# A ViT tower on one core: the FFN's up products reordered, and scores and turns moved ahead

## The reference

```
h = tok(x)                                   # patches projected, width 192
qkv = layernorm(h) @ W_qkv.T
att = softmax(8 * q @ k.T); o = att @ v      # inside one image, 36 x 36, 12 heads
h = h + cat(o) @ W_out.T
g = argmax(softmax(layernorm(h) @ gate_w + gate_b))
y = gelu(layernorm(h) @ w1[g] + b1[g]) @ w2[g] + b2[g]    # 192 -> 768 -> 192
out = h + y
```

## Time and profile before

| what | value |
|---|---|
| median of 3 runs | 298.41 us (297.48 to 299.12) |
| profiled execution | 296.83 us |
| its span, first to last instruction | 295.1 us |
| mean granted TensorE clock | 0.961 |
| PE busy | 270.5 us (92%) |
| DVE, ACT, POOL busy | 133.0, 127.2, 63.9 us |
| DMA mean | 80 GB/s |

### The profile page before, as it was taken

How to read it: one execution, slowest core, us unless ns; L and a number is a source line. 1 busy time by engine, 2 the same in 40 slices (tenths; PEclk the granted TensorE clock), 3 DMA queues, 4 the chain that set the end, 5 groups by cost and what they waited for, 6 DMA issues and landing times.

```text
span 295.1 us, 9448 instructions
## 1 busy us (share of the span) xinstructions
PE 270.5 (92%) x3858; PEld 243.8 (83%) x3859; DVE 133.0 (45%) x434; ACT 127.2 (43%) x362; POOL 63.9 (22%) x105
## 2 busy tenths in 40 slices
PE   7957989999999999999999987598999999999991
PEld 7937978899879999799998777496888888898890
DVE  6986067442575742774625742353223232232210
ACT  3463543634452725526444432304746355364330
POOL 2750001212002121012120001136052442533112
PEclk9985999999999999999999979869999999999998
DMA  6929900021950302000020000204012121121000
GB/s 247 286 59 429 413 22 2 13 114 51 420 234 4 125 0 60 4 2 4 2 62 3 2 4 2 60 0 130 7 53 67 40 55 58 47 48 42 10 0 0
DMA packets 5169, 23.47 MB, mean 80 GB/s; under 512 B 1383, under 2 KB 2675, under 8 KB 4878
## 3 DMA queue, kind: packets, MB, share of 16 engines
q1 hardware_dynamic: 3038, 18.48, 17.2%
q0 software_dynamic: 1792, 4.04, 5.0%
q10 hardware_dynamic: 304, 0.44, 0.5%
HBM read 20.30 MB, written 3.34 MB: 80 GB/s over the span
## 4 chain that ended last, share of the span: by engine, by line
PE 84%; DVE 6%; ACT 3%; issue 3%; POOL 1%; DMA 1%; POOLq 0%; DVEq 0%; ACTq 0%
PE psum L403 19%; PE psum L681 11%; PE psum L665 9%; PE psum L473 9%; PE psum L669 7%; PE psum L388 6%; PE psum L448 5%; PE psum L462 4%; PE psum L511 4%; PE psum L434 2%; PE psum L535 2%; PE psum L653 1%; PE psum L522 1%; DVE kT L943 1%; PE psum L396 1%
## 5 line engine op out<-in xcount | busy, mean ns | idle before, releaser
L862 ACT ACTIVATE kT<-psum,late 128x128 f32<-128x128 f32 x96 | 26.5, 375 | 43.8 <-PE psum L669 43.8
L403 PE MATMUL psum<-xn_hi,wq_parts 128*128 128x288 f32 x144 | 36.6, 324 | 3.0 <-DVE late_r L916 3.0
L1194 POOL TENSOR_SCALAR veps<-mv 96x1 f32<-96x1 f32 x24 | 5.3, 219 | 148.4 <-DVE mv L896 148.2
L681 PE MATMUL psum<-w2s,kT 128*128 x192 | 33.8, 327 | 0.0
L665 PE MATMUL psum<-qT,late 128*128 128x128 f32 x192 | 32.6, 292 | 0.0
L681 PEld LDWEIGHTS psum<-w2s,kT 128*128 128x128 f32 x192 | 30.8, 190 | 0.1
L403 PEld LDWEIGHTS psum<-xn_hi,wq_parts 128*128 128x128 f32 x144 | 26.4, 204 | 3.3 <-issue 3.3
L665 PEld LDWEIGHTS psum<-qT,late 128*128 128x128 f32 x192 | 25.8, 190 | 4.0
L403 PE MATMUL psum<-late_r,wq_parts 128*128 128x288 f32 x96 | 29.0, 310 | 0.0
L473 PE MATMUL psum<-wo,oT 128*96 128x192 f32 x144 | 27.3, 342 | 1.7 <-ACT oT L775 1.7
L403 PE MATMUL psum<-wq_parts,xn_hi 128*100 128x384 f32 x96 | 28.4, 350 | 0.0
(11 more groups left out here) (133 smaller groups left out, 473.5 us busy)
## 6 DMA issues: line engine op xcount, KB each, us to landing
w1s<-w_b SPq DMA_DIRECT2D x1, 4632.0 KB, 16.5
w2s<-w SPq DMA_DIRECT2D x1, 4608.0 KB, 15.7
xb<-xT SPq DMA_DIRECT2D x4, 864.0 KB, 4.5
token_table<-rows SPq DMA_DIRECT2D x3, 432.0 KB, 3.2
late<-w_proj SPq DMA_DIRECT2D x1, 960.0 KB, 4.9
b2s<-b SPq DMA_DIRECT2D x1, 768.0 KB, 17.8
wq_in<-w_qkv SPq DMA_DIRECT2D x1, 640.0 KB, 9.7
wo<-w_out SPq DMA_DIRECT2D x1, 576.0 KB
```

The lines of the kernel that those rows point to most:

```text
L403: mm = pe.matmul(dst, lhsT, rhs, start=(i == 0), stop=(i == len(parts) - 1))
L681: mm = pe.matmul(psum[:, Y_BANKS[i % 2], 0:D], hidT[i % 2][:, c * P:(c + 1) * P], w2s[:, bass.ds(e, 1), c, :], start=(c == 0), stop=(c == ...
L862: ge = act.activation(hidT[p2][:, c * P:(c + 1) * P], psum[:, 2 * p2 + c % 2, c // 2 * P:(c // 2 + 1) * P], ACT.Gelu, bias=w1_tile[i][:, U ...
```

## The change

Five edits. (1) `up` issues the 6 full-row products first and then the 6 half-row ones; for the first FFN tile the second tile's `turn_x` stands between the two. (2) `soften(1)` stands ahead of `normalise(0)` on DVE. (3) `scores(3)` stands ahead of the last `values`. (4) In the last block `turn_probs(3)` and `attend(2)` stand ahead of `project_to(0)`, and on ACT `take_attended(3)` ahead of `take_rows(0)`; the bank list follows. (5) 14 fillers instead of 24 ahead of the sorting product.

```
-FINAL = [("o", 0), ("gt", 0), ("o", 1), ("o", 2), ("gt", 1), ("gt", 2)]
+FINAL = [("o", 0), ("o", 1), ("gt", 0), ("o", 2), ("gt", 1), ("gt", 2)]
...
-                if n in (0, 2, 4, 7):
+                if n in (0, 2, 4):
...
-                    scores({0: 0, 2: 1, 4: 2, 7: 3}[n], 0)
+                    scores(n // 2, 0)
                 if n == 6:
                     turn_probs(0, 0)
+                    scores(3, 0)
...
                     attend(0, b)
                     attend_next(1)
+                    attend_next(2)
                     project_to(0)
-                    attend_next(2)
                     attend(3, b)
...
                 ranks(b)
+                scores(3, b + 1)
                 next_values((3, 1))
-                scores(3, b + 1)
...
-                for c in range(0, FCH, 2):
+                for c in range(FCH):
                     at = c // 2 * P
-                    for k in range(2):
-                        pe.matmul(psum[:, 2 * p2 + k, at:at + SLOT], wA[:, (c + k) * P:(c + k + 1) * P], fxA[p2],
-                                  start=True, stop=False)
-                    for k in range(2):
-                        rows_ = slice(DB * k, DB * (k + 1))
-                        mm = pe.matmul(psum[:, 2 * p2 + k, at:at + SLOT], wB[rows_, at:at + P], fxB[p2][rows_, :],
-                                       start=False, stop=True)
+                    pe.matmul(psum[:, 2 * p2 + c % 2, at:at + SLOT], wA[:, c * P:(c + 1) * P], fxA[p2],
+                              start=(c < 2), stop=False)
+                if between is not None:
+                    between()
+                for c in range(FCH):
+                    at, half = c // 2 * P, slice(DB * (c % 2), DB * (c % 2 + 1))
+                    mm = pe.matmul(psum[:, 2 * p2 + c % 2, at:at + SLOT], wB[half, at:at + P], fxB[p2][half, :],
+                                   start=False, stop=(c >= FCH - 2))
...
-            keep_clock(24, TR_BANK)
+            keep_clock(14, TR_BANK)
...
             turn_x(0, 0)
-            turn_x(0, 1)
-            up(0, 0)
+            up(0, 0, lambda: turn_x(0, 1))
...
                     take_attended(2, b)
+                    take_attended(3, b)
                     take_rows(0)
-                    take_attended(3, b)
...
                 soften(0, b)
+                soften(1, b)
                 normalise(0, b)
-                soften(1, b)
                 soften(2, b)
```

More of the change, by code:

```diff
@@ L654, in turn_x, with up @@
                 pe.transpose(dst[0:DB, SLOT:2 * SLOT], xg[i % 4][:, D + DA:2 * D], ident[:, :]).then_inc(fxt_full, 1)
-            def up(r, i):
+            def up(r, i, between=None):
                 j, p2 = r * 4 + i, i % 2
```

## The result

Beside runs of the kernel before on the same chip, the changed kernel takes 283.12 us (4 runs, 279.88 to 284.55) against 298.76 (4 runs, 297.48 to 300.83). The ratio is 0.940 (95% interval 0.929 to 0.951); it leaves the two slower ones of the four runs out, so it is not the quotient of the medians, and the profiled execution, at 284.33, is one of these two. In two later measurements the changed kernel stood at 0.945 (0.939 to 0.952) and 0.946 (0.943 to 0.949), with medians of 281.88 and 281.42. The gain is 15.6 us by the medians above, 18 by their ratio, and 16 by each of the two later ratios; 20.0 were forecast. The change is faster, and the time lies in the range, but 2 to 4 us of the forecast gain are missing.

A forecast was written before the change was run, and what follows sets the result against it. PE alone was taken to bound the FFN, 29% of the span. Terms 12.8 + 1.9 + 5.0 + 0.3 = 20.0 us took 296.8 to 276.8; the 1.6 offset to the runs' median gave 278.4, range 275.5 to 285.0.

The forecast's parts named there:

- Rival A: Up: half-row runs don't hide weight loads, each step stays 0.21 us; FFN saves 6.5, not 12.8; 284.7 us; chance 0.12.
- the rule on weight loads: Trainium skill's rule on packed small matmuls: a weight load overlaps running products only where the row group differs.
- Rival D: Up: halves don't run side by side in the long run; FFN saves 2.4 us, time 289; chance 0.03.
- The FFN's 12.8: FFN: 15 of 16 tiles save 0.81 us each in up, 12.2, plus 0.6 for the first.
- 1.9 were summed: soften(1) ahead of normalise(0): PE's wait before the third scores goes, 1.24 us, plus 0.7 for two later blocks.
- That is 5.0 us: Last block: `turn_rows(2)` at 183.6 instead of 188.59, from an earlier start, ACT waits removed and `project_to(0)` at full clock.
- a third one: Last block: a third PE wait for ACT's copies, about 0.7 us, expected to go.
- The start of `attend(0)`, counted at 1.0: Last block: `attend(0)` starts at 168.9 instead of 169.91, as unit 3's scores come earlier.
- Its bounds were 3.4 and 5.0: Last block's saving: 3.4 us if the clock falls again, 5.0 if not; 5.0 was taken.
- 0.3 was taken between 0.8 and -2.4: Fillers: sorting starts up to 0.8 us earlier, but a late clock rise may lose 2.4; 0.3 gain taken.
- Rival B: Clock falls again in the last block (1.6 us) and rises late after the fillers (1.8 more): 281.8 us; chance 0.17.
- forecast at 7.2: Everything except the up: softmax order, scores ahead, last block's order and fillers together, predicted to bring 7.2 us.

The follow-up runs named there:

- halves_apart: The changed kernel with the six half-row products ordered 0, 2, 4, then 1, 3, 5 instead of alternating halves: 288.10 us (2 runs).
- after_again: The changed kernel itself, unaltered, measured a second time in a later job: 281.88 us, ratio 0.945 to the kernel before.
- after: The changed kernel's profile from its first measurement: median 283.12 us, ratio 0.940 to the kernel before; the profiled execution took 284.33.
- after_third: The changed kernel itself, unaltered, measured a third time as its job's yardstick: 281.42 us, ratio 0.946 to the kernel before.
- old_last: The changed kernel with the last block's old order on PE and ACT and the old bank list: 279.86 us, ratio 0.938 to the kernel before.
- spread: The changed kernel with project_to(0) back before the last turn, and between turn_probs(3) and attend(2) in the first three blocks; ACT's swap kept: 281.39 us, ratio 0.946.
- act_swap_only: The changed kernel with project_to(0) back between attend(1) and the last turn, keeping ACT's swap and the new bank list: 281.00 us, ratio 0.943.

## Why the prediction was right in its direction and 2 to 4 us too high in its gain

**Up.** Right, in mechanism and size. Full rows were forecast at 1.42 and took 1.43; half rows at 0.86 and took 0.87. The disputed bound was the price of a half-row step inside a run: 0.11 was taken, 0.11 came. Rival A (0.21) is out, and with it the rule on weight loads that stood behind it, at least for these products. Rival D is out; `halves_apart` shows what lost alternation costs. The FFN's 12.8 came as 12.5 in the profile, and the up alone as 11.4 in the medians and 12.1 by the ratio.

**soften(1) ahead.** Right. The waits of the earlier trace rows are gone in the opening and in the transitions; the third unit's scores start at 40.84, 1.2 us earlier:

```profile
40.57 0.34 PE L403 MATMUL psum<-wq_parts,late_r 128*100 128x384 f32 x1
40.84 0.65 PE L434 MATMUL psum<-kT,qT 64*36 64x36 f32 x48
```

In the profile of `after_again`, where no fall of the clock stands in these blocks, block 3's tokens start at 125.7 instead of 128.2. Counted from the first scores, that is 2.2 earlier, where 1.9 were summed.

**The last block.** This is the step that failed: "That is 5.0 us", of which 0.71 and 0.96 for ACT's waits, 0.7 for a third one, and 1.5 for a projection at the full clock. The waits did go. But I priced six groups of small products in a row by PE's time alone, so the wait for the program stood in the sum at nothing, and the clock at its better bound. Such groups use up instructions faster than 16 KB blocks arrive, and stops of 1.0 to 1.7 us stood in the place of the waits in all eight profiles of the new order. The projection ran at the full clock in one of them only: `project_to(0)`, named at 2.0 us, took 3.8 in `after`, 3.3 in `after_again` and 2.2 in `after_third`. The start of `attend(0)`, counted at 1.0, came as 0.8: 0.36 and 0.45.

The lines that mark the stretches below, of before and of `after_again`:

```profile
128.23 0.40 PE L388 MATMUL psum<-late,xb 128*96 128x192 f32 x1
```

```profile
125.70 0.49 PE L388 MATMUL psum<-late,xb 128*96 128x192 f32 x2
183.98 0.27 PE L396 MATMUL psum<-ident,rows 96*128 96x96 f32 x1 [0.42 <-DVE rows L901]
199.01 0.27 PE L654 MATMUL psum<-ident,xb 128*128 128x128 f32 x1
```

Taken between such starts, in us, with the three profiles of the changed kernel:

| stretch | before | saving forecast | `after` | `after_again` | `after_third` |
|---|---|---|---|---|---|
| first scores to block 3's tokens | 92.5 | 1.9 | 94.0 | 90.3 | 92.4 |
| from there to `turn_rows(2)` | 60.4 | 5.0 | 58.5 | 58.3 | 56.6 |
| from there to the first `turn_x` | 13.6 | 0.3 | 13.8 | 15.0 | 13.0 |
| from there to the last down's end | 86.4 | 12.8 | 74.0 | 74.0 | 74.0 |

So the term of 5.0 was worth 1.9 and 2.1 with the clock's fall and 3.8 without it. Its bounds were 3.4 and 5.0; both are missed by 1.2 to 1.6, and the stops there are of 1.1 to 1.4. What the new order is worth beside the old one, with all else new and no fall in either, is seen from `turn_probs(0)` to `turn_rows(2)`: 20.9 in `old_last`, 20.4 in `spread` (which has ACT's swap) and 19.8 in `after_third`, single profiles all. With a fall behind `attend(2)` or later it is 21.7 in `act_swap_only` and 21.5 in `after_again`. So the move on PE brings 0.2 to 0.6 us and the swap on ACT 0.5, which the medians can't tell from nothing.

**Fillers.** 0.3 was taken between 0.8 and -2.4; the medians can't tell it from zero. Both ends are in the profiles: 0.6 gained in `after_third`, where the clock rose early, and 1.4 lost in `after_again`, where the 30 fillers took 6.38 us instead of 3.50.

**The clock.** Rival B had the fall in the last block and the late rise, 3.4 us in all, and 281.8. In `after_again` both came: the rise cost 1.7 against the forecast (1.8 in B), and the last block fell short of B's 3.4 by 1.3, near its stop of 1.2. Two of the three medians, 281.88 and 281.42, lie at B's time, so B describes these runs better than the forecast does; what it lacks is the stop. What no rival had is the fall near 57 us: it is why the first stretch takes 94.0 in `after` instead of 90.3, and in the changed kernel's profiles `turn_rows(2)` is at 188 with both falls, and at 184 with one of them. What decides in a given execution whether the clock falls was not settled: the same kernel shows it and doesn't show it.

Taken together, all but the up were forecast at 7.2 and brought 2.6 by the medians and 3.4 by the ratio. That covers the missing 2 to 4 us.

## What to carry to other kernels

Count how often an engine's array is switched between full-row and half-row products, and group each kind; here a round trip cost 0.4 us, and half-row products that don't alternate between the halves cost 0.32 a tile. A run of many tiny products can be bound by the supply of instructions, as here, where PE used up 16 KB in 2.7 us. Before removing a small wait between such groups, price the stop that may take its place: look at pauses marked "issue" and at the packets of the instruction queue. And where a kernel's time hangs on falls of the clock, price a term with the fall and without it, as the bounds of the prediction did, and don't take the better bound without a reason.

## What was not expected of the hardware

PE goes on 1.2 to 1.5 us after the end of a 16 KB packet of instructions, in all 26 stops of over 0.3 us. Moving the program by 256 instructions leaves the stops at the same records, and by 128 moves them; 32 tiny products in a place where PE waits anyway made the kernel some 4 us slower by the ratios. An execution of the same kernel differs by up to 5.6 us (281.22 to 286.80), and where two profiles can be compared, most of the difference lies in falls of PE's clock: at 57 to 64 us the low level cost about 4 us (block 2's tokens start at 90.1 in one profile of the changed kernel, at 85.9 in another).
